# Four graph layers on one core: the hyperedge gather's index list is counted by edge inside the dense pass, and the records by source are gathered into place

## The chip, the cores and the metric

One Trainium2 chip, one core of it. The time is the device time of one execution in microseconds, the median of several runs. The kernel's output is the table of 100000 nodes.

## The reference, cut to what matters

`x` is (100000, 128) in fp32; there are 25000 edges with `src` and `dst`, sorted by `dst`. Four layers follow each other, each on `h = relu(layernorm(x))`, each added to `x`:

```python
# L0, GCN:        x += segment_sum(w_e * (h @ W0)[dst], src) + b0
# L1, GAT:        h1 = (leaky(h) @ W1.T + b1) @ Wg.T; coeff = softmax by dst of leaky(a_src[src] + a_dst[dst])
#                 x += leaky(segment_sum(h1[src] * coeff, dst) + bias_g) @ W2.T + b2
# L2, hypergraph: d_v = clip(segment_sum(hw[he], node), 1); he = segment_sum((h / sqrt(d_v))[node], he)
#                 x += (segment_sum((he * hw / d_e)[he], node) / sqrt(d_v)) @ L2_W.T + L2_b   # node = src, he = dst
# L3, tensor product of spherical parts, edge network on 8 attributes, segment_sum by dst
#                 x += output_linear(segment_sum(features(h[src], attr), dst))
```

The input of a row that no edge touches is only shifted by the biases; the kernel does that in a dense pass over all rows and corrects the rows that edges touch.

## The kernel before, in words

Edges are padded to 25088 and tiled as 196 tiles of 128 edges, four tiles to a group, 49 groups. Loops over groups (`for_groups`) have four groups written out, a loop of eleven turns of four, and a last group. A stage ends when all five queues (SP, POOL, PE, ACT, DVE) have counted up one semaphore (`stage_end`). DVE orders its dependent instructions by a semaphore of its own (`done`, `need`, `link`). All indirect DMAs are POOL's, one for a tile: it moves one row for each of 128 edges. `L291` in waits is the line of `stage_end`.

Stage 1. ACT and SP load the inputs, DVE sorts the edges' source keys (15 rounds on 128 x 256 keys, with PE turning them); five chunks of the dense pass and the flags and targets by dst are put between its rounds (`meanwhile`). `unpack` then writes `idx_e_s` (the edge number of each place in the order by source) and the sorted keys `keyl`. The **dense pass** goes over the 781 rows of each partition in 71 chunks of 11 rows: SP loads a chunk (`load_chunk`, L509), DVE copies three vectors into it and adds the bias sum C (`dense_chunk`, L434 to L437), SP stores it (L514). There are five buffers. After the sort, DVE does 60 chunks in a loop (`dense_steps`), then six more with the flags by src between them, then the rest rows (`dense_left`). Meanwhile POOL gathers the records by source (`gathers("BY_SRC", ...)`, L681): 196 gathers of 64-byte records from `rec_d` into a ring of four groups, and ACT copies four words of each into `rec_s` (`keep_records`, L1149). DVE waits for the last of these copies, casts two columns into `idx_dst_s` and `idx_last_s` (L1716, L1717), and ends the stage.

Stage 2, GCN and the list. POOL gathers 196 tiles of the table by `idx_dst_s` (L681) and then adds 196 tiles into it by `idx_add_s` (L695), each group as soon as ACT has kept it. DVE, ACT and PE work on each group between (L1772 subtracts, L1734 and L1724 statistics, L1748 running sums; PE L893 to L907; ACT L1203, L1226, L1210, L1218 `keep`). When all groups are kept, DVE makes the **list** `idx_run_d` for the hyperedge gather of stage 6, which needs, by edge in the order by dst, where the run of its source node lies in the order by dst. That is done in two loops over the groups:

- the ranks: SP loads 512 source keys in sorted order, broadcast to 98 partitions (L559); DVE compares them with the lanes of the dst keys (`steps`, L1820, L1821); PE turns the steps into windows of 128 keys (`rank`, L927, L928: 16 matmuls); DVE counts equal keys (`counts`, four L1830 and two L1832) and ACT the smaller ones (`signs`, L1250);
- some 13 instructions of arithmetic on 128 x 196 (L1847 to L1859) make the list in the order by source;
- placing: DVE makes two one-hot matrices a tile (`onehot`, L1865, L1866) and PE multiplies them (`place`, L937) into one bank, which holds the list in the order by edge; five more instructions (L1880 to L1885) split it into rows.

Stage 3 is GAT up to the logits (two gathers a tile, L742); stage 4 the softmax coefficients; stage 5 GAT's sums (POOL multiplies, L753); stage 6 the hyperedge sums (gathers by `idx_run_d`, L681); stage 7 their way back, with one-hots and placing of another list beside it (gathers of `he`, L681, adds, L695); stage 8 the last layer (gathers of `s2`, adds).

Of the kernel before, what the change touches and what calls it, by code (L numbers as in the profile page):

```python
# [29 lines left out]
P = 128  # L30
TILES = math.ceil(E / P)
# [129 lines left out]
def build_gnn(nc, x, src, dst, edge_attr_4, edge_attr_8, edge_weight, node_vec1, node_vec1_n2,  # L161
# [8 lines left out]
    rec_d = nc.dram_tensor("rec_d", (EP, REC), fp32).ap()  # L170
# [11 lines left out]
    with ctx:  # L182
# [15 lines left out]
        key_col = {k: sb(f"key_{k}", [P, TILES]) for k in ("dst", "src")}  # L198
# [83 lines left out]
        recs_ready, recs_stored = sem("recs_ready"), sem("recs_stored")  # L282
        exp_asked, exp_done = sem("exp_asked"), sem("exp_done")
# [34 lines left out]
        MAPS = loop_sems("maps", "step ranked counted signed onehot placed")  # L318
# [49 lines left out]
        dl, kp = work[0:LANES, 0:256], work[0:LANES, 256:512]  # L368
        jump_e, jump_o = work[0:LANES, 512:641], work[0:LANES, 644:773]
        step_e = [work[0:LANES, 6496 + k * 512:7008 + k * 512] for k in range(2)]  # L370
        step_o = [work[0:LANES, 9584 + k * 512:10096 + k * 512] for k in range(2)]
        junk = ring(1024, 128, 8)
        iota_f = work[:, 10880:11136]
        n_sign, n_eq, n_blk, row_f, col_f, run_f, tmp_c = (work[:, 11136 + k * TILES:11136 + (k + 1) * TILES] for k in range(7))
        place_r = ring(2400, GROUP * TILES)
        hot_r = ring(5536, 512)
# [90 lines left out]
        def _(sp):  # L467
# [80 lines left out]
            sp.wait_ge(lanes_free, 1)  # L548
            k = keys_dram["dst"]
            sp.dma_start(dl, k[1:EP + 1].rearrange("(q f) -> q f", f=F)).then_inc(lanes_in, 16)  # L550
            sp.dma_start(kp[1:LANES, :], k[F + 1 - P:EP + 1 - P].rearrange("(q f) -> q f", f=F)).then_inc(lanes_in, 16)
            for_groups(sp, lambda G: load_flags(sp, G, "src", GCN))

            def load_keys(G):
                if G.from_(UNROLL):
                    sp.wait_ge(MAPS["step"], G.g - (UNROLL - 1))
                k = keys_dram["src"]
                part = k[bass.ds(G.g * GE + 1, GE)] if not isinstance(G.g, int) else k[G.g * GE + 1:(G.g + 1) * GE + 1]
# [93 lines left out]
        def _(pool):  # L652
# [15 lines left out]
            def gathers(name, table_ap, of, free=None, columns=ROW, ring_=rows_r, done_before=0):  # L668

                def body(G):  # L670
                    if G.from_(UNROLL):
                        if free is None:
                            rows_in.wait(pool, name, G.before(UNROLL))
                        else:
                            pool.wait_ge(free, G.g + (done_before - UNROLL + 1))
# [51 lines left out]
            every_group(gathers("BY_SRC", rec_d, [idx["e_s"]], R["taken"], REC, done_before=NG))  # L727
# [60 lines left out]
        def _(pe):  # L788
# [81 lines left out]
            sort_transposes(runs_by_dst)  # L870
            to_cols(fa)
            carries(1, bwd_row)
            to_cols(fa)
            to_cols(fa)
# [43 lines left out]


            def rank(G):  # L920
                pe.wait_ge(MAPS["step"], G.g + 1)
                if G.from_(UNROLL):
                    pe.wait_ge(MAPS["signed"], G.g - (UNROLL - 1))
                for t in range(GROUP):
                    c = slice(t * P, (t + 1) * P)
# [194 lines left out]
        def _(act):  # L1120
# [123 lines left out]
            def signs(G):  # L1244
                if G.from_(1):
                    act.wait_ge(MAPS["signed"], G.g)
# [902 lines left out]
```

## Time and profile before

| | us |
|---|---|
| median of 3 runs | 3422.17 (3417.45 to 3425.61) |
| span of the profiled execution | 3771.4 |
| busy in it: POOL, DVE, PE, ACT | 2419.5, 1939.4, 1698.6, 996.4 |
| idle before the first gather of stage 3 | 129.6 |
| HBM read and written | 243.25 MB and 175.32 MB |

The page gives no time of the profiled execution other than its span. The span runs from the first to the last instruction; the runs' times are taken without the profiler. Busy times leave out waits. A row of the timeline has the start, the duration, the engine, the line and the operation, and in brackets the idle time before it with what ended it; "issue" is idle time for which the trace shows no releaser.

### The profile page before, as it was taken

What the parts mean: (1) busy time and instruction counts of PE and PEld (TensorE: products, weight loads), DVE (VectorE), ACT (ScalarE), POOL (GpSimd) and SP (SyncE); (2) the same over time, 40 slices, a digit from 0 to 9 for tenths busy, and PEclk for the clock granted to TensorE, in tenths of its full rate; (3) what the DMA queues carried; (4) which work ended last, traced back from release to release, by engine and by line L of the source; (5) the groups of instructions that cost most, each with busy time, mean ns of one, the idle gap of its engine ahead of it and who ended that gap; (6) DMA issues with size and microseconds to landing.
All of it is one profiled execution on the core that took longest, in us unless ns stands there. A gap on an engine that the chain in (4) does not pass through costs nothing. (4 is left out here: it accounts for less than half of the span.)

```text
span 3771.4 us, 39244 instructions
## 1 busy us (share of the span) xinstructions
PE 1698.6 (45%) x7728; PEld 1270.6 (34%) x7728; DVE 1939.4 (51%) x6174; ACT 996.4 (26%) x2804; POOL 2419.5 (64%) x2037
## 2 busy tenths in 40 slices
PE   0100011158887433534425423257677764555553
PEld 0000010046776311211115312235455543555553
DVE  5755310058889634434455545543333335766664
ACT  0000010046652033434413334432222222211211
POOL 0088777768881366666504466548888886888887
PEclk9999995578899866677755555566666666767766
DMA  2799522235571122222228534446655554555555
GB/s 86 113 404 417 206 48 55 52 42 60 62 114 26 25 63 62 72 62 69 59 82 260 181 92 102 97 96 115 114 112 115 111 114 101 123 116 110 116 114 78
DMA packets 331651, 419.35 MB, mean 111 GB/s; under 512 B 81230, under 2 KB 244867, under 8 KB 331269
## 3 DMA queue, kind: packets, MB, share of 16 engines
q0 software_dynamic: 128576, 119.75, 21.9%
q1 hardware_dynamic: 156988, 258.63, 20.6%
q10 hardware_dynamic: 46028, 40.40, 4.7%
q14 instruction: 47, 0.39, 0.0%
q8 instruction: 12, 0.20, 0.0%
HBM read 243.25 MB, written 175.32 MB: 111 GB/s over the span
## 5 line engine op out<-in xcount | busy, mean ns | idle before, releaser
L1748 DVE TENSOR_TENSOR_SCAN work<-work,bank 128x512 f32<-128x512 bf16 (+1 forms) x294 | 363.9, 1263 | 435.7 <-PE bank L882 265.8
L742 POOL DMA_INDIRECT big<-out_dram,idx_src_d x196 | 193.2, 986 | 277.5 <-DVEq L291 129.6
L695 POOL DMA_INDIRECT out_dram<-big,idx_add_s x196 | 310.1, 1582 | 83.4 <-issue 55.1
L695 POOL DMA_INDIRECT out_dram<-big,idx_add_d x196 | 313.3, 1598 | 77.2 <-issue 58.8
L695 POOL DMA_INDIRECT out_dram<-work,idx_add_s x196 | 316.6, 1615 | 70.6 <-issue 58.2
L681 POOL DMA_INDIRECT work<-rec_d,idx_e_s x196 | 252.0, 1286 | 169.5 <-DVE idx_e_s L1510 110.1
L1210 ACT ACTIVATE work<-work 128x128 f32<-128x128 f32 x784 | 317.4, 481 | 138.2 <-DVE work L1743 114.1
L1203 ACT ACTIVATE work<-work,eps_col 128x4 f32<-128x4 f32 (+1 forms) x196 | 58.5, 299 | 885.9 <-DVE work L1724 435.2
L681 POOL DMA_INDIRECT work<-d,idx_run_d x196 | 191.7, 978 | 133.3 <-DVE big L1991 63.2
L882 PE MATMUL bank<-ident,work 128*128 128x128 f32 x392 | 105.3, 421 | 364.5 <-ACT work L1210 140.2
L951 PE MATMUL bank<-ident,work 128*128 128x128 f32 x392 | 81.7, 377 | 373.8 <-ACT work L1210 256.8
L681 POOL DMA_INDIRECT work<-he,idx_last_s x196 | 192.1, 980 | 87.5 <-issue 59.5
L681 POOL DMA_INDIRECT big<-out_dram,idx_dst_s x196 | 192.2, 981 | 63.4 <-issue 63.1
L681 POOL DMA_INDIRECT work<-s,idx_e_d x196 | 191.1, 975 | 62.0 <-issue 59.5
L742 POOL DMA_INDIRECT work<-out_dram,idx_dst_d x196 | 190.7, 973 | 59.8 <-issue 59.8
L951 PEld LDWEIGHTS bank<-ident,work 128*128 128x128 f32 x392 | 64.8, 195 | 419.1 <-issue 216.1
L882 PEld LDWEIGHTS bank<-ident,work 128*128 128x128 f32 x392 | 68.0, 210 | 398.1 <-issue 182.9
L753 POOL TENSOR_TENSOR work<-work 128x512 f32<-128x512 f32 x49 | 68.9, 1406 | 192.0 <-DMA work<-gat_coefficients 182.2
L1734 DVE BATCH_NORM_STATS2 work<-work 128x6 f32<-128x128 f32 x784 | 166.4, 279 | 14.4 <-remote 8.9
L1865 DVE TENSOR_SCALAR work<-work 128x128 f32<-128x128 f32 x392 | 112.9, 288 | 112.0 <-PE bank L1050 102.7
L893 PE MATMUL bank<-work 128*128 128x128 f32 x392 | 72.8, 330 | 215.9 <-ACT work L1210 139.5
L1073 PE MATMUL bank<-ident,work 128*128 128x128 f32 x196 | 50.3, 406 | 241.5 <-ACT work L1210 204.7
(333 smaller groups left out, 4994.0 us busy)
## 6 DMA issues: line engine op xcount, KB each, us to landing
out_dram<-big SPq DMA_DIRECT2D x71, 726.0 KB
big<-in_x_dram SPq DMA_DIRECT2D x71, 704.0 KB, 11.2
edge_w<-work SPq DMA_DIRECT2D x49, 512.0 KB
work<-edge_w ACTq DMA_DIRECT2D x49, 512.0 KB
work<-flags_src SPq DMA_DIRECT2D x98, 128.0 KB
gat_h<-work SPq DMA_DIRECT2D x49, 256.0 KB
work<-flags_dst SPq DMA_DIRECT2D x98, 128.0 KB
work<-gat_h SPq DMA_DIRECT2D x49, 256.0 KB, 3.9
```

Source lines behind the costliest of these rows:

```text
L681: g_.indirect_dma_start(to, None, table_ap, bass.IndirectOffsetOnAxis(ap=f[:, at_:at_ + 1], axis=0)).then_inc(of_rows(name).of(G), 16)
L695: g_.indirect_dma_start(table[:, :], bass.IndirectOffsetOnAxis(ap=of[:, at_:at_ + 1], axis=0), row, None, compute_op=ALU.add).then_inc(add ...
L742: g_.indirect_dma_start(to[:, t * ROW:(t + 1) * ROW], None, table, bass.IndirectOffsetOnAxis(ap=of[:, at_:at_ + 1], axis=0)).then_inc(rows ...
L753: g_.tensor_tensor(h_r[G.slot], in_r[G.place], co_r[G.place], ALU.mult).then_inc(GATSUM["h"], 1)
L882: last = T.transpose(out[:, t * P:(t + 1) * P], of[:, t * P:(t + 1) * P], ident[:, :])
L893: T.matmul(bank[G.slot][:, c], h_r[G.slot][:, c], diag_r[G.slot][:, c], start=True, stop=True)
L951: last = T.transpose(bank[2 * G.slot + t // 4][:, t % 4 * P:(t % 4 + 1) * P], h8[G.slot][:, t * P:(t + 1) * P], ident[:, :])
L1203: S_.activation(s[:, 104:104 + tiles], s[:, 81:81 + 2 * tiles:2], ACT.Sqrt, bias=eps_col[:, :]).then_inc(S["dev"], 1)
L1210: last = S_.activation(h[:, t * P:(t + 1) * P], v(t), ACT.Relu, bias=stat[:, 8 + t:9 + t], scale=stat[:, t:t + 1])
L1734: done(V.bn_stats(s[:, 16 + 6 * t:22 + 6 * t], v(t)))
L1748: return V.tensor_tensor_scan(to, flag_b[G.place][rows, :], of, before if G.from_(1) else 0.0, ALU.mult, ALU.add)
L1865: done(V.tensor_scalar(hot[:, t * P:(t + 1) * P], iota[:, 0:P], row[:, t:t + 1], None, ALU.is_equal))
```

## The change

The list is counted in the order by edge, so the places need no one-hots. The source keys are stored by edge in DRAM (`src_by_edge`) and loaded by ACT instead of SP; the ranks' loop lies inside the dense pass of stage 1, four groups to a step of five chunks; the arithmetic follows it. The stage-2 loops for ranks and placing are gone, as are `key_src` and its transpose. `rec_d` has 4 instead of 16 words a record, and POOL gathers each tile straight into its columns of `rec_s`, waiting for its own gather of four groups before; ACT's copies are gone. Buffers are laid elsewhere in `work`. In stage 2 SP loads flags alone. `onehot` stays for stage 7 and only moves. The diff, cut:

```diff
-    rec_d = nc.dram_tensor("rec_d", (EP, REC), fp32).ap()
+    rec_d = nc.dram_tensor("rec_d", (EP, 4), fp32).ap()
+    src_dram = nc.dram_tensor("src_by_edge", (EP,), fp32).ap()
...
+        def keys_of(G):
+            return cols4(rec, G, GROUP * REC).rearrange("p (t c) -> p t c", c=REC)[:, :, R_SRC]
...
@@ sync, stage 2
-            sp.wait_ge(lanes_free, 1)
-            sp.dma_start(dl, ...).then_inc(lanes_in, 16)
-            sp.dma_start(kp[1:LANES, :], ...).then_inc(lanes_in, 16)
             for_groups(sp, lambda G: load_flags(sp, G, "src", GCN))
-            def load_keys(G):
-                if G.from_(UNROLL):
-                    sp.wait_ge(MAPS["step"], G.g - (UNROLL - 1))
-                sp.dma_start(flag_r[G.place][0:LANES, :], part.partition_broadcast(LANES)).then_inc(keys_at.of(G), 16)
-            sp.wait_ge(GCN["chained"], NG)
-            for_groups(sp, load_keys)
@@ gpsimd, stage 1
-            every_group(gathers("BY_SRC", rec_d, [idx["e_s"]], R["taken"], REC, done_before=NG))
+            def records(G):
+                if G.from_(UNROLL):
+                    rows_in.wait(pool, "BY_SRC", G.before(UNROLL))
+                for t in range(GROUP):
+                    at_ = G.g * GROUP + t
+                    g_.indirect_dma_start(rec_s[:, 4 * at_:4 * at_ + 4], None, rec_d,
+                                          bass.IndirectOffsetOnAxis(ap=idx["e_s"][:, at_:at_ + 1], axis=0)
+                                          ).then_inc(rows_in.of(G), 16)
+            every_group(records)
@@ tensor: rank moves from stage 2 to stage 1, place goes
             sort_transposes(runs_by_dst)
+            for_groups(pe, rank)
             to_cols(fa)
             carries(1, bwd_row)
             to_cols(fa)
-            to_cols(fa)
+            pe.wait_ge(MAPS["signed"], NG)
             stage_end(pe, 1)
...
-            pe.wait_ge(GCN["kept"], NG)
-            for_groups(pe, rank)
-            pe.wait_ge(MAPS["signed"], NG)
-            for_groups(pe, place)
@@ scalar, stage 1
             neighbours("dst", 1)
+            act.wait_ge(lanes_free, 1)
+            act.dma_start(dl, ...).then_inc(lanes_in, 16)
+            act.dma_start(kp[1:LANES, :], ...).then_inc(lanes_in, 16)
+            act.wait_ge(src_ready, 1)
+            act.dma_start(src_dram.rearrange("(q f) -> q f", f=F), key_f[0:LANES, :]).then_inc(src_stored, 16)
+            act.wait_ge(src_stored, 16)
             store_flags("dst", 1)
...
             neighbours("src", 2)
-            keep_records("BY_SRC", rec_s, 4)
-            act.wait_ge(R["taken"], 2 * NG)
+            def load_keys(G):
+                if G.from_(UNROLL):
+                    act.wait_ge(MAPS["step"], G.g - (UNROLL - 1))
+                part = src_dram[...]
+                act.dma_start(key_r[G.place][0:LANES, :], part.partition_broadcast(LANES)).then_inc(keys_at.of(G), 16)
+            def body(G):
+                load_keys(G)
+                if G.from_(3):
+                    signs(G.before(3))
+            for_groups(act, body)
+            for g in (NG - 3, NG - 2, NG - 1):
+                signs(group(g))
+            act.wait_ge(MAPS["signed"], NG)
             store_flags("src", 3)
@@ vector, stage 1
-            dense_steps(SORT_STEPS, STEPS - 1)
-            dense_one(0)
+            dve.wait_ge(lanes_in, 32)
...
+            def dense_and_ranks(i):
+                for q in range(DBUF):
+                    dense_chunk(V, dve, i, q)
+                    if q < UNROLL:
+                        G = Group(i - 1, q)
+                        steps(G)
+                        if G.from_(1):
+                            counts(G.before())
+            dense_and_ranks(1)
+            with dve.Fori(2, STEPS - 1) as i:
+                ...
+                dense_and_ranks(i)
+            steps(group(NG - 1))
+            counts(group(NG - 2))
+            dense_one(0)
             counts(group(NG - 1))
             dve.wait_ge(MAPS["counted"], NG)
             dve.wait_ge(MAPS["signed"], NG)
             ...
-            for_groups(dve, onehots, order)
-            dve.wait_ge(MAPS["placed"], NG)
-            link(V.tensor_copy(run_d, bank[4][:, 0:TILES]))
+            link(V.tensor_copy(run_d, run_f))
             ...
+            dve.wait_ge(keys_in, 64)
+            run_flags(keyl, prevl, nextl, "src")
+            dense_one(1)
...
-            to_cols(V.tensor_copy(fa, keyl), key_col["src"][:, :])
             dense_one(4)
             dense_one(5)
             dense_left()
-            dve.wait_ge(R["taken"], 2 * NG)
+            rows_in.wait_all(dve, "BY_SRC")
```

## Rows read from the trace of the kernel before

**Rows 1.** The page: its first line, and the busy time by engine.

```profile
span 3771.4 us, 39244 instructions
...
PE 1698.6 (45%) x7728; PEld 1270.6 (34%) x7728; DVE 1939.4 (51%) x6174; ACT 996.4 (26%) x2804; POOL 2419.5 (64%) x2037
```

**Rows 2.** POOL by line: min/median/max ns of one, first and last start.

```profile
L681 POOL DMA_INDIRECT work<-rec_d,idx_e_s x196: 943/947/2314, 185.6 to 496.1; - x196
L681 POOL DMA_INDIRECT big<-out_dram,idx_dst_s x196: 942/947/1792, 500.4 to 750.8; - x196
L681 POOL DMA_INDIRECT work<-d,idx_run_d x196: 942/947/1462, 2142.0 to 2451.7; - x196
L681 POOL DMA_INDIRECT work<-he,idx_last_s x196: 943/958/1250, 2481.2 to 3088.9; - x196
...
L742 POOL DMA_INDIRECT work<-out_dram,idx_dst_d x196: 943/947/1601, 1280.7 to 1866.2; - x196
...
L695 POOL DMA_INDIRECT out_dram<-big,idx_add_s x196: 1560/1562/2071, 755.3 to 1144.5; - x196
```

**Rows 3.** Waits of POOL: us in total, times (first row: and longest).

```profile
POOL big L742 <- DVEq L291: 129.6, 1, 129.6
...
  DVE sc_d L1907: 84.7, 13
...
  DVE big L1991: 63.2, 11
```

**Rows 4.** Timeline of stage 2, PE and ACT: start us, us, what.

```profile
563.60 0.16 PE L907 MATMUL bank<-one,work 1*128 1x1 f32 x1 [2.64 <-issue]
...
668.61 0.59 ACT L1218 COPY big<-bank 128x512 f32<-128x512 f32 x1 [83.68 <-remote]
```

**Rows 5.** Timeline of DVE: two GCN groups; the list's ends.

```profile
894.45 0.69 DVE L1772 TENSOR_TENSOR work<-big,w_C 128x512 f32<-128x512 f32 x1 [0.22 <-issue]
...
899.83 0.69 DVE L1772 TENSOR_TENSOR work<-big,w_C 128x512 f32<-128x512 f32 x1 [0.35 <-PE bank L895]
...
1036.97 0.37 DVE L1798 TENSOR_SCALAR dvis_s<-big 128x196 f32<-128x196 f32 x1 [4.64 <-ACT big L1219]
...
1274.93 0.36 DVE L1885 TENSOR_TENSOR idx_run_d<-idx_run_d,work 128x196 int32<-128x196 int32 x1
```

**Rows 6.** The chain, its first piece of stage 4.

```profile
1904.12 4.09 DMA work<-gat_logits
```

**Rows 7.** Lines of POOL: 755 to 1010, 1010 to 1310, 2481 to 3100 us.

```profile
L695 POOL DMA_INDIRECT out_dram<-big,idx_add_s x125 | 197.0, 1576 | 61.8 <-issue 35.3 <-ACT big L1219 21.9 <-DMA big<-out_dram,idx_dst_s 2.7
...
L695 POOL DMA_INDIRECT out_dram<-big,idx_add_s x72 | 114.7, 1593 | 21.9 <-issue 20.1 <-DMA out_dram<-big,idx_add_s 1.5 <-ACT big L1219 0.3
...
L681 POOL DMA_INDIRECT work<-he,idx_last_s x196 | 192.1, 980 | 87.5 <-issue 59.5 <-SPq L291 28.0
```

**Rows 8.** Timeline of DVE at the end of stage 1.

```profile
498.54 0.33 DVE L1716 CAST idx_dst_s<-rec_s 128x196 int32<-128x196 f32 x1 [75.08 <-ACT rec_s L1149]
```

**Rows 9.** Lines of DVE, 1010 to 1310 us: busy us, mean ns, idle.

```profile
L1830 DVE TENSOR_SCALAR_CACHE_REDUCE work<-bank,key_src 128x128 f32<-128x128 f32 x196 | 56.9, 345 | 11.4 <-PE bank L928 6.9 <-issue 3.4
...
L1820 DVE TENSOR_SCALAR work<-work 98x512 f32<-98x512 f32 x49 | 24.2, 494 | 1.6 <-issue 1.6
```

**Rows 10.** Lines of DVE, the dense pass, 187 to 398 us.

```profile
L437 DVE TENSOR_TENSOR big<-big,w_C 128x1408 f32<-128x1408 f32 x61 | 98.7, 1617 | 0.0
...
L434 DVE COPY big<-big 128x11 f32 x60 | 12.6, 210 | 91.8 <-DMA big<-in_x_dram 91.2 <-DVE work L1517 0.6
```

**Rows 11.** Windows: PE, PEld, DVE, ACT, POOL busy; PEclk, DMA share, GB/s.

```profile
187.00:400.00 213.00, 0.00 (x0) 0.00 (x0) 120.14 (x250) 7.19 (x30) 176.39 (x121) 1.00 1.01 408
...
755.00:1010.00 255.00, 194.35 (x1282) 157.12 (x1281) 194.12 (x611) 150.02 (x451) 195.66 (x125) 0.82 0.48 54
...
1033.00:1146.00 113.00, 93.31 (x700) 85.55 (x700) 97.52 (x519) 62.83 (x331) 95.03 (x60) 0.93 0.71 118
```

**Rows 12.** Lines of POOL, 180 to 400 us.

```profile
L681 POOL DMA_INDIRECT work<-rec_d,idx_e_s x122 | 177.9, 1458 | 147.0 <-DVE idx_e_s L1510 110.1 <-issue 36.9
```

More of the change, by code:

```diff
@@ L870, in _, with rank @@
             sort_transposes(runs_by_dst)
+            def rank(G):
+                pe.wait_ge(MAPS["step"], G.g + 1)
+                if G.from_(UNROLL):
+                    pe.wait_ge(MAPS["signed"], G.g - (UNROLL - 1))
+                for t in range(GROUP):
+                    c = slice(t * P, (t + 1) * P)
+                    o = bank[2 * G.place + t // 2][:, t % 2 * F:t % 2 * F + P + 1]
+                    T.matmul(o, step_e[G.slot][:, c], jump_e, start=True, stop=False)
+                    last = T.matmul(o, step_o[G.slot][:, c], jump_o, start=False, stop=True)
+                last.then_inc(MAPS["ranked"], 1)
+            for_groups(pe, rank)
             to_cols(fa)
@@ L1582, in targets @@
                 to_cols(V.tensor_tensor(fa, fa, trash, ALU.add), add_idx[:, :])
-            def dense_steps(first, last):
-                with dve.Fori(first, last) as i:
-                    for q in range(DBUF):
-                        dense_chunk(V, dve, i, q)
             def dense_one(n):
@@ new lines, in counts @@
+            def counts(G):
+                dve.wait_ge(MAPS["ranked"], G.g + 1)
+                need(order.off)
+                eq, blk = (cols4(c, G) for c in (n_eq, n_blk))
+                key = keys_of(G)
+                for t in range(GROUP):
+                    w = bank[2 * G.place + t // 2][:, t % 2 * F:t % 2 * F + P]
+                    done(V.tensor_scalar(junk[t], w, key[:, t:t + 1], None, ALU.is_equal, ALU.add, accum_out=eq[:, t:t + 1]))
+                for k in range(2):
+                    ins = V.tensor_copy(blk[:, 2 * k:2 * k + 2], bank[2 * G.place + k][:, P:2 * F:F])
+                    if k == 0:
+                        done(ins)
+                ins.then_inc(MAPS["counted"], 1)
@@ new lines, in dense_and_ranks @@
+            def dense_and_ranks(i):
[4 more added lines that the diff above has]
+                        steps(G)
+                        if G.from_(1):
+                            counts(G.before())
+            assert SORT_STEPS == 1 and (STEPS - 2) * UNROLL == NG - 1
+            dense_and_ranks(1)
+            first, each = order.off, UNROLL * 6
+            with dve.Fori(2, STEPS - 1) as i:
+                order.base, order.off = i * each - 2 * each, first
+                dense_and_ranks(i)
+                assert order.off == first + each
@@ new lines, in _ @@
+            order.base, order.off = 0, first + (STEPS - 3) * each
+            steps(group(NG - 1))
+            counts(group(NG - 2))
+            dense_one(0)
+            counts(group(NG - 1))
+            need(order.off)
+            dve.wait_ge(MAPS["counted"], NG)
+            dve.wait_ge(MAPS["signed"], NG)
+            link(V.tensor_tensor(n_sign, n_sign, n_eq, ALU.add))
+            link(V.tensor_scalar(n_sign, n_sign, 0.5, float(P // 2 - P - 1), ALU.mult, ALU.add))
+            link(V.scalar_tensor_tensor(run_f, n_blk, float(P), n_sign, ALU.mult, ALU.add))
@@ L2039, in _, with onehot @@
             link(V.tensor_copy(col_s, to_int(place_s[:, 0:TILES])))
+            def onehot(G, hot, place, iota, row_c, col_c, of_c):
+                row, col, of = (cols4(c, G) for c in (row_c, col_c, of_c))
+                for t in range(GROUP):
+                    done(V.tensor_scalar(hot[:, t * P:(t + 1) * P], iota[:, 0:P], row[:, t:t + 1], None, ALU.is_equal))
+                    ins = V.tensor_scalar(place[:, t * TILES:(t + 1) * TILES], iota[:, 0:TILES], col[:, t:t + 1], of[:, t:t + 1],
+                                          ALU.is_equal, ALU.mult)
+                    if t < GROUP - 1:
+                        done(ins)
+                need(order.off)
+                return ins
             def body(G):
```

180 lines of the change are left out of this document (58 added, 122 removed).

## The prediction

> **What bounds the kernel now.** I first read the page's head [rows 1]: the span is 3771.4 us and POOL is busy for 2419.5 of them, more than any other engine. Its instructions are almost all indirect DMAs, 196 per gather or add. A gather takes 0.947 us, an add 1.56 us [rows 2], and each is followed by about 0.30 us of issue (the gathers from 500.4 to 750.8 us start 1.28 us apart), so 1.25 and 1.87 us apiece where nothing disturbs them.
>
> The median of the runs is 3422.2 us, 349 us less than this execution's span. The page gives no other time for the profiled execution, so 3771 is taken as its own time. An edit inside a stretch that exists in the profiled execution alone is worth nothing in the runs, so I look for the 349 us first. POOL waited 129.6 us for DVE ahead of stage 3, 84.7 us in thirteen waits within stage 3 and 63.2 us in eleven waits within stage 6 [rows 3]: 277 us. The rest can lie behind the last gathers of stages 3 and 6 and in late adds. These waits grow out of one pattern. During the gathers of stage 2, PE starts a tiny matmul only after 2.64 us in which nothing but "issue" is named as its reason, again and again; ACT then waits 83.7 us for what PE should have made [rows 4]. Later in the same stage, with POOL at its adds, a whole group takes DVE 5.4 us (899.83 less 894.45) [rows 5]. The same code runs many times faster once the gathers are over, and I read the crawl as something that the profiled execution adds. Set every stage to POOL's own pace and the sum comes close to the runs' median: stage 1 ends at 500; stage 2 takes 196 x 1.25 for gathers, 196 x 1.88 for adds and 8 for its ends, 621; stage 3 takes 392 x 1.25 + 15 = 505; stage 6 takes 196 x 1.25 + 15 = 260; and the rest as profiled, from some 1900 to 2142 and from 2481 to the end, 1532 in all [rows 2, 6]. That is 3418.
>
> The Trainium skill, in "NOTIFIC — the notification-queue block", the section on overflow, says that a full notification ring can be set to stall the engine that feeds it. No run here shows whether that happened; the sum doesn't use it, and it would speak for A against B below.
>
> **Stage 2, where work is removed.** The list for the later gather starts on DVE at 1036.97 and ends at 1275.3 [rows 5]: 238 us, about half of it ranks, the rest one-hots and placing. The adds on POOL end at 1146 [rows 2], and the next gather starts only after the 129.6 us wait [rows 3]. In the profiled execution the list is thus the end of stage 2, and without it the wait shrinks to a landing and a barrier, some 4 us: 126 us less.
>
> In the runs, by the reading above, the GCN groups keep up with the gathers (5.4 us against 4 x 1.25 = 5.0), so they end some 25 us after the last gather, near 780. The list would end at 780 + 238 = 1018. The adds run from 755 for 196 x 1.88 = 368 us, to 1123. The list has 105 us to spare, and taking it away brings nothing by itself. Even if a group took 6.5 us (318 in all, to about 835) it would end at 1073. I take 0, and keep 126 as the other end.
>
> Taking DVE's work from beside the adds could give a little: adds beside GCN groups take 1.576, beside the list 1.593 us [rows 7], against the undisturbed 1.560 [rows 2]. 0.033 us on the 63 adds that ranks cover is 2 us; no row excludes as much again from the one-hots. I take -2, bounds -5 and 0.
>
> **Stage 1, where work is added.** It ends with the gather of records, first issued at 185.6, last at 496.1 [rows 2]; DVE has waited 75.1 us for the last record to be copied by ACT when it goes on at 498.54 [rows 8]. So DVE may finish 75 us later at no cost. What lands on it: 48 groups of ranks inside twelve steps of five chunks, one group and the closing arithmetic behind them. By the means of one, L1820 and L1821 take 0.5 us each and four L1830 0.345 each [rows 9], 2.4 us a group with what overlaps set against copies and waits; 48 groups are 113 to 115 us. The 60 chunks took 209 us, in which DVE sat idle 92 us for chunks to arrive [rows 10], so a chunk costs it 1.95. If all idle time is used, DVE is some 21 us later; if none, 113. But the DMA engines are full there, share 1.01 at 408 GB/s [rows 11]. The 49 key loads (196 KB each, broadcast) move into this stretch, off SP's queue onto ACT's. The share was 0.48 beside adds alone, 0.71 with some 47 key loads in 113 us [rows 11]: 0.55 us of all 16 engines a load, 27 us together. So a step needs 17.4 + 2.2 = 19.6 us of DMA and 5 x 1.95 + 4 x 2.4 = 19.4 us of DVE. Two loads this even get in each other's way: I take 20.5 us a step, 37 us more. The closing arithmetic (19 short instructions of 128x196) and the last group add 9, the dropped transpose of the keys gives 1 back. DVE is ready 45 us later, at 469, before POOL's 498. The new waits: DVE waits for keys ahead of each group and, behind them, for PE; queued there are the dense adds, for which SP's loads and stores wait. ACT issues a key load two to three groups ahead of its use, some 10 us, and four activations of signs stand between two loads. PE has 16 small matmuls a group and did nothing here before. The two lane loads and the 98 KB store of src stand on ACT's queue ahead of the flags, during the sort, where ACT has nothing else: 0. SP loses loads in stage 2 that nobody waited for by then: 0.
>
> POOL itself: 196 gathers before and after, the same instruction; its wait is now for its own landing four groups back instead of ACT's copy, no tighter. The last copy falls away: -0.3. But its pace in the dense pass matters. A gather takes 1.458 us there [rows 12] and 0.947 alone: the dense add of 1.62 us [rows 10] holds it up, a good 1.0 us per chunk, and the number of chunks beside the gathers stays. What ranks do to gathers isn't in the trace. The nearest row: gathers beside one-hots in stage 7 take 0.980 [rows 7], 0.033 over the free pace, so 0.033 x 196 = 6 us; below, zero. If L1820 and L1821 blocked for their whole length, it were 98 x 0.4 = 39 us. I take +3, nearer the one-hots, since they are the same kind of instruction.
>
> The Trainium skill ("SBUF — State Buffer", the section on the shared port pair) says that VectorE's two-port modes, or two SBUF inputs, lock GpSimd out for the whole instruction. By the dense add, 1.458 against 0.947, the trace agrees; by the one-hots, fp32 from SBUF to SBUF too, at 0.980, it hardly does. By that rule in full the ranks would cost the 39 us.
>
> **Sum.** Stage 1: -0.3 + 3; stage 2: -2; no other stage is touched. That is +1 us on the median, 3423.
>
> **Rivals.**
> A, the forecast: both ends are POOL's, before and after. For it: the sum of 3418, the 75 and 105 us of slack. Own range 3414 to 3433. Chance 0.55.
> B, faster: the list is exposed in the runs too, as in the profile. For it: the plain wait of 129.6 us [rows 3]. Against: then the missing 349 us have no place. 3422 - 126 = 3296. Chance 0.18.
> C, slower: the dense pass becomes the end of stage 1. Its place is DVE's in-order queue, behind keys, PE and chunks; it decides once the step exceeds 17.4 + (75 - 8) / 12 = 23.0 us. With no idle time used (113), 8 of arithmetic and half of the 27 us of key loads, DVE is 134 us later, 59 over the slack: 3481; halfway there it is 3450. Chance 0.13.
> D, slower: ranks block the gathers. At half of the 39 us it is 3442, in full 3461. It decides where ranks cost a gather over 0.05 us on the mean. Chance 0.09.
> The last 0.05 is for a small gain, adds less disturbed than bounded or 16-byte gathers landing sooner: 3412.
>
> **Numbers.** 0.2% is 6.8 us, about what a measurement of this kernel can tell from no change. In A, 0.50 of 0.55 stay within it, 0.03 above and 0.02 below. Faster: 0.18 + 0.05 + 0.02 = 0.25. Slower: 0.13 + 0.09 + 0.03 = 0.25. Same: 0.50. B, far off, stays out of the range; it takes in the small gain and nearly all of C and D, 3408 to 3480.
>
> **What would show it.** Right: stage 1's last gather still near 496 and DVE's last wait there down from 75 to about 30 us; POOL's wait ahead of stage 3 down from 129.6 to some 4 us in the profile while the median hardly moves; the span falls by about 126 us unless PE crawls beside the gathers of stage 1, where it has work now. Wrong: a median near 3300 (B: the crawl is in the runs too), DVE last in stage 1 with waits for keys (C), or gathers beside ranks well above their 1.458 us (D).

## The result and the profile after

The kernel after takes 3407.7 us (median of 6 runs, 3398.5 to 3418.4), the kernel before, run beside it, 3421.6 us (6 runs, 3417.5 to 3428.5). The ratio is 0.9958, with a 95% interval from 0.9945 to 0.9971: 14 us faster, where 3423 was forecast in a range from 3408 up and a chance of 0.25 was given to faster.

The head of the page of the kernel after, against [rows 1]:

```profile
span 3396.4 us, 37399 instructions
...
PE 1667.8 (49%) x7334; PEld 1259.3 (37%) x7334; DVE 1835.4 (54%) x5774; ACT 980.2 (29%) x2755; POOL 2380.7 (70%) x2037
```

This execution took 3398.5 us in all, the shortest of the six runs. The kernel before had a span of 3771.4 us; the profiled executions of the kernel after and of all the kernels below lie within 13 us of their medians. So the extra 349 us were that one execution's, as reading A took it, and the wait of 129.6 us [rows 3] went with them. They must not be read as a gain of the change.

POOL's lines of the kernel after (columns: busy us, mean ns | idle us before, by releaser), against [rows 2, 7]:

```profile
L685 POOL DMA_INDIRECT out_dram<-big,idx_add_s x196 | 306.3, 1563 | 62.2 <-issue 54.5 <-DMA out_dram<-big,idx_add_s 4.9 <-DMA big<-out_dram,idx_dst_s 2.8
L723 POOL DMA_INDIRECT rec_s<-rec_d,idx_e_s x196 | 229.7, 1172 | 182.1 <-DMA rec_d<-rec 122.7 <-issue 59.4
L741 POOL DMA_INDIRECT big<-out_dram,idx_src_d x196 | 196.0, 1000 | 62.0 <-issue 59.4 <-POOLq L293 2.6
```

Three readings. The record gathers take 1.172 us on the mean, before 1.286 (252.0 us for the 196): 22 us less. But they now wait for the table's store, not for the index, and the first starts at 198.1 us instead of 185.6 [rows 2]. The adds of stage 2 take 1.563 us, and stage 3 begins 2.6 us behind them.

The issue of that store in the kernels before and after (last column: median us to landing):

```profile
rec_d<-rec ACTq DMA_DIRECT2D x1, 1568.0 KB, 20.8
```

```profile
rec_d<-rec ACTq DMA_DIRECT2D x1, 392.0 KB, 54.5
```

A quarter of the bytes takes 34 us longer to land. Issued at 143.31, it lands at 197.8.

The end of stage 1 in the timeline of the kernel after, against [rows 8]:

```profile
484.70 0.27 DVE L1601 TENSOR_TENSOR big<-big,w_C 32x128 f32<-32x128 f32 x1
...
486.09 0.44 SPq L544 DMA_DIRECT2D d<-big  x1
486.30 0.94 POOL L723 DMA_INDIRECT rec_s<-rec_d,idx_e_s  x1 [0.30 <-issue]
490.84 0.33 DVE L1788 CAST idx_dst_s<-rec_s 128x196 int32<-128x196 f32 x1 [5.87 <-DMA rec_s<-rec_d,idx_e_s]
...
491.87 0.94 POOL L671 DMA_INDIRECT big<-out_dram,idx_dst_s  x1 [4.63 <-DVEq L293]
```

Stage 2 begins 8.5 us earlier than in [rows 2] (491.87 against 500.4). DVE has only 5.9 us to spare where it had 75.1, and SP's last stores stand behind DVE's last add at 484.70: both ends of the stage are now together.

Last, what a gather meets in the dense pass. Timeline of the kernel before (start us, us, what):

```profile
300.79 1.62 DVE L437 TENSOR_TENSOR big<-big,w_C 128x1408 f32<-128x1408 f32 x1
301.21 2.01 POOL L681 DMA_INDIRECT work<-rec_d,idx_e_s  x1 [0.30 <-issue]
303.53 0.94 POOL L681 DMA_INDIRECT work<-rec_d,idx_e_s  x1 [0.30 <-issue]
...
304.55 1.62 DVE L437 TENSOR_TENSOR big<-big,w_C 128x1408 f32<-128x1408 f32 x1
304.78 2.21 POOL L681 DMA_INDIRECT work<-rec_d,idx_e_s  x1 [0.30 <-issue]
```

and of the kernel after:

```profile
306.83 1.61 DVE L441 TENSOR_TENSOR big<-big,w_C 128x1408 f32<-128x1408 f32 x1
307.96 1.39 POOL L723 DMA_INDIRECT rec_s<-rec_d,idx_e_s  x1 [0.30 <-issue]
...
309.66 0.94 POOL L723 DMA_INDIRECT rec_s<-rec_d,idx_e_s  x1 [0.30 <-issue]
...
310.91 0.95 POOL L723 DMA_INDIRECT rec_s<-rec_d,idx_e_s  x1 [0.30 <-issue]
310.94 1.62 DVE L441 TENSOR_TENSOR big<-big,w_C 128x1408 f32<-128x1408 f32 x1
312.16 1.32 POOL L723 DMA_INDIRECT rec_s<-rec_d,idx_e_s  x1 [0.30 <-issue]
```

A gather that starts while a dense add runs ends 0.8 to 0.9 us behind the add's end: 301.21 + 2.01 = 303.22, the add ended at 302.41; 312.16 + 1.32 = 313.48, the add ended at 312.56. (It is 0.82 us in nearly all cases, and 0.91 us in the 48 of the kernel after in which a compare of 98x512 follows the add.) A gather that starts ahead of the add is not held up, though the add runs beside nearly all of it (310.91). And the blocked gather ties the next ones to the add: they start about 1.1 and 2.4 us behind its end, and 3.7 if there is a third. Before, the next add came 2.1 us behind the last one's end and blocked the gather at 2.4 in its first half microsecond: 2.0 to 2.2 us, two gathers a chunk. After, ranks set the dense adds about 4.2 us apart instead of 3.5 to 3.8; the add often falls just behind a gather's start, and the next gather meets only its last 0.5 us: 1.3 to 1.4 us, three gathers a chunk. Of the 67 gathers that start during a dense add, 37 start 1.0 us or more behind its start; in the kernel before none of 66 does. This is the theory that the runs had to test: **not how much DVE does beside the gathers decides, but where its long adds fall between their starts.**

### The profile page after: what moved, and what is told of

Its sections match the earlier page's. It is cut to its first block, busy times and chain, and to the rows that moved or that the text cites. A ratio compares the mean times of both kernels' runs of the same rounds, so it can differ in the third digit from the quotient of the medians.

```text
span 3396.4 us, 37399 instructions
## 1 busy us (share of the span) xinstructions
PE 1667.8 (49%) x7334; PEld 1259.3 (37%) x7334; DVE 1835.4 (54%) x5774; ACT 980.2 (29%) x2755; POOL 2380.7 (70%) x2037
## 4 chain that ended last, share of the span: by engine, by line
POOL 29%; issue 10%; PE 3%; DVE 3%; DMA 3%; ACT 1%; ACTq 1%; SPq 0%; DVEq 0%; POOLq 0%
POOL out_dram L685 18%; POOL work L671 11%; PE bank L893 1%; DMA work<-gat_coefficients 1%; ACT work L1226 1%; PE bank L973 1%; DVE work L1949 0%; POOL work L752 0%; DMA work<-flags_dst 0%; DVE work L1820 0%; PE bank L1036 0%; DVE work L1986 0%; DVE work L1987 0%; DVE work L1985 0%; DVE work L1930 0%
## 5 line engine op out<-in xcount | busy, mean ns | idle before, releaser
L937 PE MATMUL bank<-ident,work 128*128 128x128 f32 x392 | 96.4, 427 | 588.5 <-ACT work L1226 588.5
L723 POOL DMA_INDIRECT rec_s<-rec_d,idx_e_s x196 | 229.7, 1172 | 182.1 <-DMA rec_d<-rec 122.7
L685 POOL DMA_INDIRECT out_dram<-big,idx_add_s x196 | 306.3, 1563 | 62.2 <-issue 54.5
L1888 DVE TENSOR_TENSOR work<-big,w_K 128x512 f32<-128x512 f32 x49 | 33.9, 692 | 542.5 <-DMA work<-out_dram,idx_dst_d 542.5
L937 PEld LDWEIGHTS bank<-ident,work 128*128 128x128 f32 x392 | 76.9, 223 | 635.2 <-issue 424.3
L893 PE MATMUL bank<-ident,work 128*128 128x128 f32 x392 | 104.3, 418 | 301.4 <-ACT work L1226 170.2
L671 POOL DMA_INDIRECT work<-d,idx_run_d x196 | 186.5, 952 | 73.3 <-issue 59.4
L893 PEld LDWEIGHTS bank<-ident,work 128*128 128x128 f32 x392 | 67.0, 208 | 334.2 <-ACT work L1226 128.5
L878 PE MATMUL bank<-work 98*128 98x129 f32 x392 | 129.6, 432 | 87.2 <-DVE work L1712 86.9
L1059 PE MATMUL bank<-ident,work 128*128 128x128 f32 x196 | 49.7, 402 | 247.3 <-ACT work L1226 247.3
```

What stands on the lines that cost most here:

```text
L671: g_.indirect_dma_start(to, None, table_ap, bass.IndirectOffsetOnAxis(ap=f[:, at_:at_ + 1], axis=0)).then_inc(of_rows(name).of(G), 16)
L685: g_.indirect_dma_start(table[:, :], bass.IndirectOffsetOnAxis(ap=of[:, at_:at_ + 1], axis=0), row, None, compute_op=ALU.add).then_inc(add ...
L723: g_.indirect_dma_start(rec_s[:, 4 * at_:4 * at_ + 4], None, rec_d, bass.IndirectOffsetOnAxis(ap=idx["e_s"][:, at_:at_ + 1], axis=0)).then ...
L878: T.matmul(o, step_e[G.slot][:, c], jump_e, start=True, stop=False)
L893: last = T.transpose(out[:, t * P:(t + 1) * P], of[:, t * P:(t + 1) * P], ident[:, :])
L937: last = T.transpose(bank[2 * G.slot + t // 4][:, t % 4 * P:(t % 4 + 1) * P], h8[G.slot][:, t * P:(t + 1) * P], ident[:, :])
```

## The experiments

All kernels ran in turns with the kernel before on their chip; its median was 3418.7 us in experiments 1, 2, 3 and 5, 3424.1 in 4, 6, 7 and 8 (`after_halves`), and 3418.4 in 9 (`after_turned_halves`) to 12. Ratios are to that one. "Dense add" is DVE's instruction in the dense pass; the adds of stage 2 are POOL's indirect DMAs.

**1. No list.** The kernel before without the list of stage 2.

```
-            for_groups(sp, load_keys)        # SP, and PE's rank and place, ACT's signs
...
-            for_groups(dve, body, order)     # steps, counts, one-hots
...
+            link(V.tensor_copy(idx["run_d"][:, :], idx["e_s"][:, :]))
```

> The kernel before with the whole list of stage 2 left out (key loads, ranks, signs, one-hots, placing); the later gather of the sums takes a permutation of the edges as its index list instead, so it fetches other rows. Theory 1, the list is hidden in the runs: 0 to -5 us (adds of stage 2 at about 1.56 instead of 1.59 us each), 3417 to 3422. Rival, the list is where the measured 14 us come from: about 3408. Rival, the profile's wait of 129.6 us exists in the runs too: near 3296.

Measured: 3409.0 us, ratio 0.9970 (0.9958 to 0.9982), 10 us less. Twice what theory 1 allowed, and nothing like 126. The reason is in the adds of stage 2; in this kernel, and below it in direct_narrow (experiment 2), whose list is the old one:

```profile
L682 POOL DMA_INDIRECT out_dram<-big,idx_add_s x196 | 306.3, 1563 | 62.2 <-issue 57.9 <-DMA big<-out_dram,idx_dst_s 2.8 <-DMA out_dram<-big,idx_add_s 1.5
```

```profile
L695 POOL DMA_INDIRECT out_dram<-big,idx_add_s x196 | 313.3, 1598 | 62.7 <-issue 57.9 <-DMA big<-out_dram,idx_dst_s 3.4 <-DMA out_dram<-big,idx_add_s 1.5
```

313.3 - 306.3 = 7 us of the 10; the other 3 are not placed. The list is hidden, but not free: in direct_narrow the 61 adds beside the ranks take 1.636 us on the mean and the 67 beside the one-hots 1.593, against 1.562 behind the list. How, its timeline shows:

```profile
806.72 0.47 DVE L1828 TENSOR_SCALAR work<-work 98x512 f32<-98x512 f32 x1
806.88 1.74 POOL L695 DMA_INDIRECT out_dram<-big,idx_add_s  x1 [0.30 <-issue]
808.92 1.56 POOL L695 DMA_INDIRECT out_dram<-big,idx_add_s  x1 [0.30 <-issue]
```

The compare ends at 807.19 and the add that started during it at 808.62, 1.43 us later. So do all 24 adds of this stage that start 0.08 to 0.30 us behind the start of such a compare (they end 1.43 to 1.44 us behind its end and take 1.61 to 1.84 us). A compare of 98x512 therefore holds up an indirect DMA that starts during it, as a dense add does.

**2. Records alone.** The kernel before with the narrow table and the gathers straight into place, list and ranks as they were.

```
-    rec_d = nc.dram_tensor("rec_d", (EP, REC), fp32).ap()
+    rec_d = nc.dram_tensor("rec_d", (EP, 4), fp32).ap()
...
-            every_group(gathers("BY_SRC", rec_d, [idx["e_s"]], R["taken"], REC, done_before=NG))
+            every_group(records)
...
-            keep_records("BY_SRC", rec_s, 4)
```

> The kernel before with the part on the records alone: table of 4 words an edge, 16-byte rows gathered straight into place, no copies on ACT. If the short pieces make the store late, the first gather starts near 198 instead of 185.6 us. Theory 1, the pace of the gathers is set by the dense adds: mean stays 1.286 us, stage 1 ends about 12 us later, 3432 to 3435. Rival, a shorter row or the missing copy makes the gather faster: mean near 1.17, stretch 288 us, 3411.

Measured: 3424.3 us, ratio 1.0018 (1.0009 to 1.0028), 6 us more. The first gather starts at 198.8 (wait for `rec_d<-rec` 123.2 us, landing 55.3 us); the mean is 1.258, not 1.17. Both forecasts missed: 3411 by far, and 3432 to 3435 because the mean did not stay at 1.286. Straight into place brings nothing (a gather that meets no dense add takes 0.95 us here too, and one that meets one costs 1.0 us more, as before); the late start is half given back, since four dense chunks fewer stand beside the gathers.

**3. Spaced.** The kernel before with idle arithmetic behind four of five dense chunks.

```
                     dense_chunk(V, dve, i, q)
+                    if q < UNROLL:
+                        need(order.off)
+                        pads(q)      # 2 compares 98x512, 4 of 128x128, 2 copies 128x2
```

> The kernel before with idle arithmetic behind four of five dense chunks: two compares of 98x512, four of 128x128, two small copies, as the ranks of the kernel after, but no keys, no PE, no ACT. Its results are used nowhere. Theory 1, a gather that is issued while a dense add runs waits for its end, and the ranks only set the adds further apart and in another phase to the gathers: mean falls from 1.286 to 1.15 to 1.20 us, stage 1 ends some 20 us earlier, 3395 to 3405. Rival, the compares hold gathers up as the dense adds do, and the gain has another source: mean at or above 1.286, 3421 or more.

Measured: 3425.2 us, ratio 1.0021 (1.0012 to 1.0031): slower by 7 us, mean 1.318. By its number the rival was right. But the timeline shows the theory's own rule at work, with a phase that I had guessed wrongly:

```profile
304.63 1.62 DVE L437 TENSOR_TENSOR big<-big,w_C 128x1408 f32<-128x1408 f32 x1
304.96 2.20 POOL L681 DMA_INDIRECT work<-rec_d,idx_e_s  x1 [0.30 <-issue]
...
307.47 0.94 POOL L681 DMA_INDIRECT work<-rec_d,idx_e_s  x1 [0.30 <-issue]
...
308.39 1.62 DVE L437 TENSOR_TENSOR big<-big,w_C 128x1408 f32<-128x1408 f32 x1
308.72 2.10 POOL L681 DMA_INDIRECT work<-rec_d,idx_e_s  x1 [0.30 <-issue]
```

The idle work took less than ranks do with their waits for PE. The dense adds stand 3.76 us apart, and each starts 0.33 us ahead of a gather, which then waits 1.2 us; 49 of the 66 chunks look so. The compares of 98x512 (306.17 to 307.04) run while that gather is still waiting or ending, and cost it 0.09 us; the gather at 307.47 runs beside those of 128x128 in 0.94 us. So the first half of the rival, that compares hold gathers up, isn't tested here: no gather starts during one of 98x512. The two theories now differ in sign for more idle work, so that was run.

**4. Spaced more.** One compare of 98x512 more in each pad.

```
+                done(V.tensor_scalar(pad_3[k % 2], pad_in[0:LANES, :], pad_in[0:LANES, 2:3], None, ALU.is_ge))
```

> The kernel spaced with one compare of 98x512 more behind each of four dense chunks, so with more idle work on DVE than the run that came out slower. Theory, a gather issued while a dense add runs waits for its end, and a blocked gather ties the phase of the next ones to that end: they start 1.2, 2.4 and 3.7 us behind it. In spaced the next add started 2.13 us behind it, just ahead of the second gather, which then waited 1.2 us. One compare more puts the add at about 2.53, just behind that gather's start, so that only a third one meets the last 0.5 us: mean 1.15 to 1.20 instead of 1.316, stage 1 ends at 475 to 480 unless DVE is later, 3395 to 3403. Rival, what counts is how much DVE does beside the gathers: mean 1.32 or more, 3425 to 3435.

Measured: 3391.2 us, ratio 0.9909 (0.9895 to 0.9924): 33 us under the kernel before, some 38 us under spaced, by adding work. Its timeline:

```profile
303.46 0.95 POOL L681 DMA_INDIRECT work<-rec_d,idx_e_s  x1 [0.30 <-issue]
...
303.57 1.61 DVE L437 TENSOR_TENSOR big<-big,w_C 128x1408 f32<-128x1408 f32 x1
304.71 1.39 POOL L681 DMA_INDIRECT work<-rec_d,idx_e_s  x1 [0.30 <-issue]
...
306.40 0.94 POOL L681 DMA_INDIRECT work<-rec_d,idx_e_s  x1 [0.30 <-issue]
...
307.65 0.94 POOL L681 DMA_INDIRECT work<-rec_d,idx_e_s  x1 [0.31 <-issue]
...
307.77 1.61 DVE L437 TENSOR_TENSOR big<-big,w_C 128x1408 f32<-128x1408 f32 x1
```

The add starts 0.11 us behind a gather, 48 times; the chunk's period is 4.2 us with three gathers in it, as in the kernel after. The mean falls to 1.115, and the last gather ends at 463.7. That is a larger gain than the theory's 3395 to 3403, in the direction that it named. The rival, that the amount of DVE's work decides, is excluded.

**5. Halves.** The kernel before with the dense add in two instructions.

```
-            eng.tensor_tensor(d_[:, :, 0:D], x_in[q], over(wts["C"][:, :], CHUNK), ALU.add).then_inc(dense_sum[q], 1)
...
+            eng.tensor_tensor(d_[:, 0:h, 0:D], xq[:, 0:h], over(wts["C"][:, :], h), ALU.add)
+            eng.tensor_tensor(d_[:, h:CHUNK, 0:D], xq[:, h:CHUNK], over(wts["C"][:, :], CHUNK - h), ALU.add
+                              ).then_inc(dense_sum[q], 1)
```

> The kernel before with each dense add in two instructions (5 and 6 of the 11 rows). Theory 1, a gather waits for the end of the one instruction that runs when it starts: a chunk costs the gathers a third to a half of the 1.04 us, mean 1.05 to 1.15, stage 1 ends 25 to 45 us earlier, 3375 to 3400. Rival, back to back halves leave no gap for the gather: a chunk costs as before, mean 1.28, 3420 to 3425.

Measured: 3379.3 us, ratio 0.9882 (0.9867 to 0.9898), 39 us less, mean 1.072. The gather gets in between:

```profile
305.45 0.82 DVE L439 TENSOR_TENSOR big<-big,w_C 128x640 f32<-128x640 f32 x1
305.89 1.19 POOL L685 DMA_INDIRECT work<-rec_d,idx_e_s  x1 [0.30 <-issue]
306.18 0.95 DVE L440 TENSOR_TENSOR big<-big,w_C 128x768 f32<-128x768 f32 x1
307.38 0.94 POOL L685 DMA_INDIRECT work<-rec_d,idx_e_s  x1 [0.30 <-issue]
```

It ends 0.81 us behind the end of the first half (306.27), though the second is already running. So do 39 of the 41 gathers that start during a first half; the other two started 0.11 us behind its start and ended 0.8 us behind the end of the second half. The wait is, with such exceptions, for the one instruction that runs at the gather's start. Why these two waited for both isn't shown.

**6. Late.** The kernel after with its ranks, still by edge, back behind the groups of stage 2.

```
 # SP, stage 2: load_keys from src_dram; PE: rank; ACT: signs; DVE: steps, counts, arithmetic
-            dense_and_ranks(1)
+            dense_steps(SORT_STEPS, STEPS - 1)
```

> The kernel after with the ranks back behind the groups of stage 2 and their keys back on SP's queue; still counted by edge, no one-hots, no placing, records in 16-byte rows straight into place. Theory, moving the ranks into the dense pass was worth 16 us in stage 1 by its effect on where the gathers start, and the list's removal from beside the adds 7 us: mean of the record gathers back to 1.26, adds of stage 2 at about 1.58, 3418 to 3422. Rival, the gain of stage 1 is not from the ranks' place: mean stays 1.17, about 3410.

Measured: 3429.0 us, ratio 1.0015 (1.0007 to 1.0024), 5 us over the kernel before and by the ratios 0.6%, 19 us, over the kernel after. Its record gathers:

```profile
L734 POOL DMA_INDIRECT rec_s<-rec_d,idx_e_s x196 | 245.8, 1254 | 196.9 <-DMA rec_d<-rec 137.5 <-issue 59.4
```

The mean goes back to 1.254: the pace of stage 1 did come from the ranks' place. The time is above the forecast. In the profiled execution, the slowest of the twelve (3441.6 us), the narrow store landed only after 69.3 us and the first gather started at 213.0; how late it lands in the median run isn't shown. With that store turned (experiment 10) the kernel is 6.5 us faster by the ratios. Landings of the narrow store were 54.5, 55.3, 57.1 and 69.3 us in four kernels.

**7. Turned.** The kernel after with the table laid out by partition, so that the store is one piece of 3136 bytes in each.

```
+            S_.copy(rec_s[:, :].rearrange("p (t c) -> p t c", c=4),
+                    rec[:, :].rearrange("p (t c) -> p t c", c=REC)[:, :, 0:4]).then_inc(recs_ready, 1)
+            act.wait_ge(recs_ready, 2)
-            act.dma_start(rec_d.rearrange("(t p) c -> p t c", p=P), ...
+            act.dma_start(rec_d.rearrange("(p t) c -> p (t c)", p=P), rec_s[:, :]).then_inc(recs_stored, 16)
+ # DVE, after the sort: idx["rec"] = (e & 127) * TILES + (e >> 7), three instructions
```

> The kernel after with the record table stored in one piece of 3136 bytes a partition: ACT packs the four words first, rows stand by partition, and three short DVE instructions turn the index. Theory, the store in 25088 pieces of 16 bytes landed 54.5 us after issue and held up the gathers by 12.5 us and the first key load with them: first gather near 186, DVE's wait of 17.5 us for the first keys down to a few, both ends 10 to 13 us earlier, 3395 to 3398. Rival, the step of the dense pass is bound by the DMA engines and takes up what was won: 3403 to 3408.

Measured: 3397.4 us, ratio 0.9926 (0.9914 to 0.9939), 0.32% or 11 us under the kernel after. The store:

```profile
rec_d<-rec_s ACTq DMA_DIRECT2D x1, 392.0 KB, 2.4
```

The first gather starts at 186.5, DVE waits 9.5 us for its first keys instead of 17.5. The gathers' mean is 1.212, worse than 1.172; the phase shifted again. Stage 2 begins at 486.0, 5.9 us earlier than in the kernel after; the rest of the 11 us isn't placed.

**8 and 9. Halves with the ranks in the dense pass.** The kernel after, and the turned one, with the edit of experiment 5.

> The kernel after with each dense add in two instructions. DVE is ready at 485 there, gathers end at 487. Theory, the gathers get faster (mean near 1.05) but stage 1 then ends with DVE: -3 to -6 us, 3401 to 3405. Rival, shorter waits let DVE's own step run faster too, or DVE is later by the second instruction's start: more than 10 us off, to either side.

> The kernel after with both edits. Theory, the gathers end near 455 to 465, DVE is ready near 477 and ends stage 1: 6 to 9 us under after_turned, 3388 to 3393, and slower than late_turned_halves by 10 us or more though it has less work in stage 2: ranks in the dense pass put DVE at the end of stage 1 once the gathers are fast. Rival, ranks in the dense pass cost nothing even then: as fast as late_turned_halves less the 5 us of quieter adds.

Measured: 3402.8 us, ratio 0.9946 (0.9934 to 0.9957), and 3395.2 us, ratio 0.9923 (0.9909 to 0.9936): by the ratios 4 us under the kernel after, with intervals that overlap, and next to nothing under the turned one, where 3388 to 3393 had been forecast. The gathers do get faster (means 1.097 and 1.09, last end at 475.4 and 459.9), but the stage no longer ends with them. DVE of after_halves and of after_turned_halves goes on with no wait to speak of:

```profile
488.43 0.33 DVE L1792 CAST idx_dst_s<-rec_s 128x196 int32<-128x196 f32 x1 [0.17 <-issue]
```

```profile
478.36 0.31 DVE L1801 CAST idx_dst_s<-rec_s 128x196 int32<-128x196 f32 x1
```

and POOL's wait ahead of stage 2 in the second names the leftover rows' stores on SP, behind DVE's last add:

```profile
POOL big L675 <- SPq L293: 24.2, 1, 24.2
```

The ranks are then no longer hidden: after_turned_halves is 22 us slower by the ratios than late_turned_halves below, the same kernel with its ranks in stage 2.

**10 to 12. The parts put together.** `late` with the turned table; that with halves; that with thirds (4, 4 and 3 rows).

> The kernel late (ranks by edge in stage 2) with the record table stored in one piece a partition, as in after_turned. Theory, all that late lost against the kernel before was the landing of the small pieces, 13 us in one profile and 27 in another: first gather at 186 to 187, mean near 1.27, together with somewhat quieter adds 0 to -8 us against the kernel before (3414 to 3422 on 3422). Rival, 16-byte rows or the missing copy on ACT are slower in themselves: more than 3425.

> The same with each dense add in two instructions. Theory, halves gain what they gained on the kernel before, 39 us, since DVE has slack again: last gather near 455, 3375 to 3383, so as fast as halves or a little faster (adds of stage 2). Rival, the gains don't add: 3390 or more.

> The same with each dense add in three instructions (4, 4 and 3 of 11 rows). Theory, a gather waits for no more than the end of one such instruction, about 0.3 us on the mean: mean of the gathers 1.00 to 1.04 against 1.07 with halves, 6 to 14 us faster than halves, 3363 to 3375. Rival, the starts of the extra instructions or the gathers' floor leave nothing: same as halves within 3 us.

Measured: 3417.2 us (ratio 0.9996, 0.9987 to 1.0005), 3371.6 us (0.9860, 0.9845 to 0.9875), 3375.7 us (0.9874, 0.9859 to 0.9890). The first gather of late_turned starts at 186.4, and its loss against the kernel before is gone. Its gathers' mean is 1.297, near that of before (1.286) and not the 1.27 of the forecast. Halves then bring 46 us, more than the 39 forecast, and the fastest kernel of the study, **3371.6 us, 47 us under before and by the ratios 0.98% under after**. Its record gathers:

```profile
L738 POOL DMA_INDIRECT rec_s<-rec_d,idx_rec x196 | 209.8, 1070 | 170.8 <-DVE idx_rec L1521 111.3 <-issue 59.5
```

Thirds were a miss: the mean stays at 1.068, and the last gather ends at 456.1 as with halves (456.0). A gather that meets a third starts 0.12 us behind its start in the median, with halves 0.44 us behind a half's, so it loses no less (1.38 against 1.22 us): the phase takes back what the shorter instruction gives. The 4 us it is slower are not clear of noise, since the intervals overlap.

## Why the prediction was wrong

**Right: reading A of the page.** The crawl belonged to the profiled execution, POOL sets both ends, and the list's removal is not worth 126 us (experiment 1: 10). Stage 2 was forecast at 621 us and took 619.8 (491.87 to 1111.65 in the kernel after). In direct_narrow, with the old list, the list ended at 1044.7 and POOL's adds at 1132.0, so it had 87 us to spare where 105 had been worked out.

**Wrong: "its pace in the dense pass matters ... a good 1.0 us per chunk, and the number of chunks beside the gathers stays. ... I take +3".** The step takes a chunk's price for a constant. It is 1.62 us less the lag of the blocked gather behind the add's start, and less another 0.03 to 0.13 us: on the mean 1.10 us in spaced, 1.01 in the kernel before, 0.66 in the kernel after, 0.50 in spaced_more. 66 gathers at 1.01 us less 67 at 0.66 us are the 22 us. The ranks moved the dense adds to a cheaper phase: -22 us in place of +3. That they met this phase was luck of their length, as spaced shows, whose idle work met a dearer one. The bounds had no negative end, and no row excluded one. The measured rows for it were there: [rows 2] shows gathers up to 2.3 us beside a median of 0.947, and the timeline of the same stretch would have shown that a gather's length follows from its start.

The direct price of the ranks, the other half of this step, was small for the same reason. Compares of 98x512 do hold up what starts during them (experiment 1), as rival D had it. But in the kernel after they stand right behind the dense add, where the blocked gather is waiting anyway: it ends 0.91 instead of 0.82 us behind the add, 48 times, some 4 us in all, and the one gather that starts during a compare, 0.05 us behind its start, isn't held up. In experiments 8 and 9, 41 and 45 gathers do start during one, near its end, and finish 0.81 to 0.82 us behind it.

The Trainium skill ("SBUF — State Buffer", the section "SBUF: two separate sides") says that whichever of the two instructions starts first gets the shared pair, and the other is fully blocked; for a VectorE instruction with two SBUF inputs it says so only against a GpSimd one that reads SBUF. I had used only the half on blocking, and without that condition. The runs agree that a gather (it reads its indices from SBUF) behind the dense add waits for the add's end, and that one ahead of it isn't held up. That the later one is blocked isn't seen for the dense add: 0.03 us or more behind a gather's start it still takes 1.61 to 1.62 us. It is seen for compares of 98x512: in late, ten of the eleven that start 0.51 to 0.68 us behind the start of an indirect add take 0.62 to 0.79 us instead of 0.48.

**Wrong: "the two lane loads ... 0", and the table's store with them at nothing.** The narrow store lands after 54.5 us, not 20.8: the first gather +12.5 us (experiment 2 has it alone, at 13.2), and the first keys are late with it, so that DVE waits 17.5 us. The part was named under "16-byte gathers landing sooner", but only for the gathers; the store of 25,088 pieces was not followed. By the medians of the turned table (experiment 7) it costs the kernel after 11 us, of which the profiled executions show 5.9 in stage 1.

**Mis-sized: DVE ready at 469.** It was ready at 485. The step was right (the ranks' steps ran from 207 to about 450 us, some 20 us each; 20.5 was forecast); the 16 us are the wait for the first keys: in the turned kernel that wait is 8 us shorter and DVE's last dense add ends 7.4 us earlier (477.5 against 485.0). Rival C, with its place on DVE's queue, came within 5.9 us of deciding, and in experiments 8 and 9 it does decide: there the stage ends with the dense pass and what SP stores behind it.

**Mis-sized: adds of stage 2, -2.** It was -7 (313.3 less 306.3), outside the bounds of -5 and 0. The number of adds that ranks cover was right, 63 forecast and 61 in direct_narrow. Their price was not: 0.033 us each was taken from the crawling execution, and it was 0.076 (1.636 less 1.560), 4.6 us. The one-hots, left at nothing, cost 2.2 us on 67 adds. Both come mostly from adds that start during a DVE instruction and wait for its end (experiment 1). The last 0.05 of the chances named "adds less disturbed than bounded", and that part did come; a gain by the gathers' pace was in no rival.

**The sum.** -22 by the gathers' pace, +12.5 by the late start, about +1 at the stage's end: -8.5 in stage 1. With -7 in stage 2 that is -15.5, against -14 of the medians. The stages of single executions are not surer than that: no_list has the stage 1 of before unchanged, and there the gathers' mean was 1.299 and stage 2 began at 502.8 instead of 500.4. Two things stay open: how these parts stood in the median run, since the profiled one was 9 us faster than that; and why the one profiled execution of before crawled, which no run touched.

## What to carry to other kernels

When one engine's instruction can hold up another's, a mean price per encounter is not a property of the pair. Read a stretch of timeline, find at which lag each length occurs, and ask how an edit moves the lag; an edit that adds work may then gain. The robust remedy is a shorter blocking instruction, which gained 39 us here without any tuning of phases (a third cut brought nothing more); and once it is in, work added beside it has no slack any more, so what was free in the old balance should be priced again. Look also at the number and size of a store's pieces, not only at its bytes.

## What the runs showed of the hardware

- An indirect gather on POOL that starts during a dense add of fp32 (two SBUF inputs) ends 0.82 us behind that one instruction's end, or 0.91 us where a compare of 98x512 follows, in 39 of 41 cases even where DVE's next dense add already runs (halves). One that starts ahead of the add takes 0.94 to 1.01 us, and so do two in the kernel after that start up to 0.02 us behind its start.
- A compare of 98x512 (fp32, one SBUF input, 0.47 us) holds up an indirect DMA that starts during it: in direct_narrow 24 adds of stage 2 end 1.43 to 1.44 us behind the compare's end and take 1.61 to 1.84 us instead of 1.56. The accumulating compares of 128x128 don't hold gathers up: 48 and 49 gathers that start during one in spaced and in the kernel after take 0.94 to 0.95 us.
- DVE and POOL lock into a phase, since the blocked gather's end is tied to the add's end: 49 and 48 of 66 chunks showed one lag (about 0.33 and 1.13 us) in spaced and spaced_more. 0.4 us of idle work a chunk was worth 38 us of the kernel, with the sign of a gain.
- A store of 25,088 pieces landed after 20.8 to 21.1 us at 64 bytes a piece and after 54.5 to 69.3 us at 16 bytes. Packed to 3136 bytes a partition, the same 392 KB landed in 2.4 us.
- The Trainium skill ("DMA: Bandwidth & Descriptors", the section on specifications) says that below 512 bytes a transfer is a read-modify-write. No run here shows that mechanism; that shorter pieces can cost more than their number is what these landings show.
